# Another order of the attention stage's work items, in a kernel of attention and a routed feed-forward layer

## What is computed

```python
q, k, v = x @ wq_w.T + wq_b, x @ wk_w.T + wk_b, x @ wv_w.T + wv_b     # to heads, then _rope(q), _rope(k)
k, v = repeat(k, 4), repeat(v, 4)                                     # 4 query heads share a key head
att = softmax(where(mask, q @ k.T / HD ** 0.5, -inf))
x = layernorm(x + (att @ v) @ cp_w.T + cp_b)
scores = sigmoid(x @ gate_w.T) + gate_b
weights, indices = top_k(scores, 4)                                   # weights divided by their sum
shared = silu(x @ w1_shared) * (x @ w3_shared) @ w2_shared
routed = sum_e probs_e * (silu((x @ w1_e) * (x @ w3_e)) @ w2_e)
x = layernorm(x + shared + routed)
```

## Time and profile before

| | us |
|---|---|
| median of three runs (lowest, highest) | 566.12 (565.82, 566.49) |
| the profiled execution | 566.13 |
| its span, first to last instruction | 564.4 |
| attention stage, to the last product with V | about 317.6 |
| TensorE (PE) busy in the span | 529.9 (94%) |
| VectorE (DVE) busy | 439.0 (78%) |
| ScalarE (ACT) busy | 369.7 (65%) |
| GpSimd (POOL) busy | 295.4 (52%) |

### The profile page before, as it was taken

One profiled execution on the slowest core, in us unless ns is written; L12 is line 12 of the kernel. 1 busy time (PEld: TensorE's weight loads), 2 busy tenths in 40 slices (PEclk: granted clock), 3 DMA queues, 4 the chain that ended last, 5 costly groups with the idle time before them and its releaser, 6 DMA issues.

```text
span 564.4 us, 12218 instructions
## 1 busy us (share of the span) xinstructions
PE 529.9 (94%) x3801; PEld 360.5 (64%) x3801; DVE 439.0 (78%) x1122; ACT 369.7 (65%) x831; POOL 295.4 (52%) x341
## 2 busy tenths in 40 slices
PE   8999999999999899989999898899999999999880
PEld 4646444445454354535433487799999999999760
DVE  2387989899889799999992269987787878785682
ACT  2444767787887598868688574467676767676132
POOL 5121231655313657358978773777544444545671
PEclk9999999999999899989999999999999999999996
DMA  5954174400632912321132541576444334320892
GB/s 145 172 72 58 30 194 132 83 4 20 99 82 64 210 37 60 64 78 60 41 124 76 164 139 40 166 247 209 153 134 134 112 117 127 117 88 6 315 355 74
DMA packets 53741, 64.95 MB, mean 115 GB/s; under 512 B 8123, under 2 KB 47438, under 8 KB 53680
## 3 DMA queue, kind: packets, MB, share of 16 engines
q1 hardware_dynamic: 45952, 46.45, 32.1%
q0 software_dynamic: 7104, 17.60, 8.9%
q10 hardware_dynamic: 624, 0.13, 0.1%
HBM read 32.49 MB, written 25.76 MB: 103 GB/s over the span
## 4 chain that ended last, share of the span: by engine, by line
PE 71%; DVE 13%; POOL 6%; issue 4%; ACT 2%; DMA 2%; SPq 1%; ACTq 0%; POOLq 0%; DVEq 0%
PE psH L1670 14%; PE psS L1475 10%; PE psO L1460 9%; PE psT L1445 8%; PE psS L1537 4%; POOL xs_scratch L753 3%; DVE MX L1139 3%; PE psG L1681 3%; PE psX L1638 3%; PE psS L1480 2%; PE psY L1693 2%; PE psY L1697 2%; PE psY L1694 2%; PE psY L1695 2%; PE psY L1696 2%
## 5 line engine op out<-in xcount | busy, mean ns | idle before, releaser
L878 ACT ACTIVATE prob<-psT 128x512 f32<-128x512 f32 (+3 forms) x384 | 167.4, 495 | 54.9 <-PE psT L1445 52.3
L1139 DVE TENSOR_REDUCE MX<-psS 128x1 f32<-128x512 f32 (+3 forms) x344 | 183.1, 595 | 11.8 <-PE psS L1480 6.0
L1475 PE MATMUL psS<-KS,QS 96*128 96x512 bf16 (+3 forms) x384 | 110.9, 330 | 4.9 <-DVE MX L1139 2.5
L824 POOL DMA_INDIRECT y_scratch<-ys,dst x80 | 77.9, 973 | 68.9 <-ACT ys L1033 54.0
L1445 PE MATMUL psT<-QS,KS 98*128 98x512 bf16 (+3 forms) x384 | 107.7, 330 | 1.8 <-DMA QS<-MT 0.9
L782 POOL TENSOR_SCALAR_AFFINE_SELECT prob<-prob 128x512 f32<-128x512 f32 x64 | 42.3, 663 | 98.1 <-ACT prob L878 97.9
L1460 PE MATMUL psO<-prob,V 128*32 128x512 f32 (+3 forms) x768 | 82.7, 505 | 1.1 <-POOL prob L782 1.0
L1670 PE MATMUL psH<-wU,xh 128*128 (+1 forms) x384 | 81.7, 334 | 0.1
L753 POOL DMA_INDIRECT xs_scratch<-x1row,slotu x64 | 65.7, 1026 | 26.9 <-issue 16.2
L1445 PEld LDWEIGHTS psT<-QS,KS 98*128 98x128 bf16 x384 | 33.9, 98 | 54.8 <-ACT prob L878 35.4
L1475 PEld LDWEIGHTS psS<-KS,QS 96*128 96x128 bf16 x384 | 37.4, 99 | 46.1 <-DVE MX L1139 23.7
(11 more groups left out here) (252 smaller groups left out, 1005.8 us busy)
## 6 DMA issues: line engine op xcount, KB each, us to landing
xs<-xs_scratch SPq DMA_DIRECT2D x80, 134.0 KB
y<-y_scratch SPq DMA_DIRECT2D x16, 512.0 KB, 10.8
QS<-qp SPq DMA_DIRECT2D x48, 128.0 KB, 5.1
wU_raw<-in_L_ffn_w_routed_dram SPq DMA_DIRECT2D x32, 176.0 KB, 3.6
xs_scratch<-padrow SPq DMA_DIRECT2D x1, 2144.0 KB
xs_scratch<-padrow SPq DMA_DIRECT2D x16, 134.0 KB
x1row<-in_L_attn_x_dram SPq DMA_DIRECT2D x4, 512.0 KB, 6.8
out_dram<-x1row SPq DMA_DIRECT2D x8, 256.0 KB, 2.8
```

Of the source, the lines that this page charges most:

```text
L824: nc.gpsimd.indirect_dma_start(y4_dram, bass.IndirectOffsetOnAxis(ap=dst[:, n % NSEL, t:t + 1], axis=0), ys[:, n % NYS, t, :], None, bound ...
L878: nc.scalar.activation(prob[:, step % NPROB, h, 0:HALF - c0], ps[:, 0:HALF - c0], ACT.Exp).then_inc(s_Tfree, 1)
L1139: nc.vector.tensor_reduce(out=MX[:, c0 // HALF, heads[0]:heads[-1] + 1, i - TH * q], in_=src, op=ALU.max, axis=AX_X).then_inc(s_Sfree, 1)
L1475: last = mm(ps[:, e * dist:e * dist + cols], QS[0:ROWS, QAT[(k // 2) % NSLOT], g % 2 * G + h, (i - TH * q) * P:(i - TH * q + 1) * P], KS[b ...
```

## The change

The nine lines of ORDER are replaced by nine others. The new string has the same letters in the same numbers, so the same 1079 items run, each stream in its own order; the interleaving is another nearly everywhere. No other line of the kernel differs, and the expert stage has the same instructions in the same order.

```diff
 ORDER = """
-aaaaaaaadadpaaldppdlpdaaaapalaaaaapaapamalpppaxxaaaxxaaxaalxxxaaxxvamaxxavxxxaaaxavaxaxpaxmaxaxaaxxaaxvxaaaxxaexpavmaaxx
+aaaaaaaaddalplaadppplaaapaaaaapaaadapaampppaxaaxaxxaaaxxaxaxaxxldvaxmaalxvxaxxaaaxaxxxavvxxewaaaxaxaxvxaawxmxaaxaxapaasd
...
 """
```

More of the change, by code:

```diff
@@ L128 @@
 ORDER = """
-aaaaaaaadadpaaldppdlpdaaaapalaaaaapaapamalpppaxxaaaxxaaxaalxxxaaxxvamaxxavxxxaaaxavaxaxpaxmaxaxaaxxaaxvxaaaxxaexpavmaaxx
[L130 to L137, removed]
+aaaaaaaaddalplaadppplaaapaaaaapaaadapaampppaxaaxaxxaaaxxaxaxaxxldvaxmaalxvxaxxaaaxaxxxavvxxewaaaxaxaxvxaawxmxaaxaxapaasd
+xavvaaxaxxalamwxaxaxaxaaxvadxaenxxaxlavaxxaxadaaxvxaxsaxxaaxavvxaxaxaexaaxpawspmaaaxdvxaxxnaxaxvxxxaaadaawxvvasxxaaxaxaa
+xasxaxnepaaavvxxaaxaaxxaxavxxaaaxaxnxpxwxavaaxraxdaamxavaxxaaaxxvdxaaxaraxxaxaxaxvvxaalexxwaaaxaxavxaaxxaxrxaxwasawxrvvx
+xxaarxxaaxvxamaaxaxanxxaxrvaxxaaaxsvvaaxxxaaxaxaaxvraaxaxxrxeaxaxaoxrvvxlaxxaaarxraaxsxavvaxxaaaxaxrwaraxmaaxxaxaxxvwvlx
+axaxaxarraxxaaxvvwxamxaxaroxaxxraexrxxvvsvxxxanaxxnxaxrxxvxmxwaaxxovxcaxxaxaaxxcxavxxlaaxcxwvvxaaxcaxeaxaxamnasxxxvvarar
+aacaxacxvxaxxaaaxxacaxaxrmxrvexaxxorxawaxxvvxxaaaxraraxxraxxarcxawcvraxvxaaxexrxrxaaxvaxrraxaxaxvlvaxxamcxanxaxxvaaxacxa
+raxearnxaasxvaaaxcxovxxwaaxaxxrscaasnaxaxxavrvexxaacacaxcxvxxwxvxxxanxaxrxaxrcvscraxaxvxxaacrxraxarawxxxaavmaxaaxsaxvrac
+axxaarxrxxsaxaavrvcxaaarreaxxsccaracrvaxxraaxsaxavwxaxaaaxrarvaxaamxaaxacxcxaasxcaxavaaxaxaxaxaraxcarxccwxvxxxvsxxccaxwa
+axvxaxxrxxveaxaxxccvxaxxvxxxvxxawacxxcaxaxxvxnmcxxvxxxcvxxxxxvcxxxrxvexxnxvxxxvxxxxcxoccccnccxxvxxcxcvxxxvxxxxxxsvvvsen
 """
```

## The result

The changed kernel took 577.98 us (median of four runs, 576.22 to 579.88), the kernel before 566.31 beside it. The ratio is 1.018, with a 95% interval from 1.013 to 1.024. The predicted time was 568.0 with a range to 572.0: the sign was right, the size was not. The profiled execution took 576.22 us with a span of 574.5.

The account below looks back on a forecast made before the run. The prediction took TensorE as the bound, with its waits and half-clock stretches the only thing an order changes. Gains of -8.8 us and costs of +10.7 summed to +1.9, from 566.1 to 568.0 us; range 561.5 to 572.

Parts of the forecast that it names:

- What bounds the kernel: TensorE, busy 529.9 of 564.4 us; an order can only change the time it waits or runs at half clock.
- Group 1's M: At 50.00 us: its small DMA, now ahead of qload 2, should take group 0's 2.6 us: -0.9.
- Group 3's M behind the pad rows: Group 3's scores wait 5.1 us for the small DMA queued behind pad rows, plus 1.4 of half clock: +6.5.
- The rule weighed: DMA descriptors are consumed in ring order, so group 3's wait is 5.1 us, 6.5 with clock; without it 561.5.
- the queue doesn't bite: Rival: group 3's small DMA gets past the pad rows, without the 6.5 us; total 561.5, chance 0.15.
- qload 6: Group 12's scores at 191.04: more TensorE items cover the load, shrinking the wait and removing half clock: -3.1.
- M of group 5: At 103.91 us: no L803 near group 5's last maximum any more, so its wait goes: -1.2.
- The route item: Second token group, 245.62 us: only one wU difference near it now, so wait and half clock go: -3.1.
- The meetings of L803: GpSimd's L803 holds VectorE at maxima of groups 6, 13, 14 and third rank: +2.4, from 0 to 6.
- slower by more: Rival: L803 meetings at group 14's last maximum and one other place cost +6.2, not +2.4; 571.8, chance 0.12.
- The shorter leads: M of group 13, its result's copy and third token group's first output transpose have less cover: +1.0, 0 to 2.
- The end: End of the attention stage: one more GpSimd scatter before the last cut, +1.3, with smaller terms: +0.8 in sum.

Follow-up runs that it names:

- the pair on one chip: Changed order as it is, 575.53 us, and with group 12's first score block moved earlier on TensorE, 577.98 us; the kernel before ran at 565.10.
- The experiment: Changed order with the split item (0,0,1) moved right behind the third split copy: 572.30 us, against 566.48 for the kernel before.
- the kernel with both edits: Changed order with the pad rows behind group 3's small DMA of M and split (0,0,1) right behind the third split: 566.14 us (before 566.35).
- group 12 earlier: Changed order with group 12's first score block three transposed scores and two products earlier: 601.00 us (before 599.55), on another chip 577.98 (before 565.10).
- the last version: Kernel with scatters in GpSimd's idle time (554.77), plus moves of ScalarE's wA copy, group 13's result copy and group 15's M: 553.98 us (before 565.10).
- group 12's blocks later: Kernel before with group 1's M ahead of qload 2 and group 12's first three score blocks three to four TensorE items later: 597.62 us (before 598.46).

## Why the prediction was wrong, step by step

- **What bounds the kernel** was right: TensorE runs the same 3801 matmuls, and the lag, its waits and half-clock stretches, makes +10.0 of the 10.1 us between the two spans.
- **Group 1's M** (-0.9): right, measured -1.0, and the same in the order of before.
- **Group 3's M behind the pad rows** (+6.5): right in every link, and shown by four edits; mis-sized by 1.5. The wait was 6.25 us and not 5.1, just over the bound of 6 that the text gave for a slow load, and the half clock behind it cost 1.8 and not 1.4. The term that was off is the rate of qload 3's transfers: 173 GB/s was taken from two us in the earlier trace rows, and 117 was found. Why one stretch has the one rate and one the other, no run asks.
- **The rule weighed** (ring order) agrees with what was measured, and the rival "the queue doesn't bite" is out: 6.25, 3.02 and no wait for 2144, 1072 and 0 KB ahead.
- **qload 6** (-3.1): right, for the right reason, the distance: 3.7 us in the traces of the pair on one chip. My experiment on its place in SP's queue was a mistake that the prediction had not made.
- **M of group 5** (-1.2), and the stretch from 60 to 215: -7.0 in all instead of -4.3. The wait for group 5's M is gone. The surplus of 2.7 us stays unexplained: between 84 and 186 us the trace of before has no other wait of TensorE over 0.05 us, so it lies in distances a little over the shortest, and I have not taken it apart.
- **The route item** (-3.1): went as said, no L1189 over 1 us, but a part of it came back at M of group 13 just behind (L1147 2.33 us, and 0.88 us of TensorE's wait at 249.56).
- **The meetings of L803** (+2.4): the step that failed most, together with the end. The prediction took the length of L803, 1.7 us, as the most that a meeting can hold VectorE, and took half of before's loss. VectorE instructions of 2.33, 2.28, 1.94 and 1.53 us came. Those of 2.33 and 2.28 are longer than any L803; the runs show for the 2.28 that the L803 behind a scatter holds VectorE from within the scatter (0.17 us with L803 not ready, 1.02 with one scatter less ahead). The 1.94 is a plain meeting, 0.42 of its own and 1.5 of hold, and the 1.53 was none with L803 at all. The rival "slower by more" named the place, the last maximum of group 14, and it happened there; behind it the clock was at half for some six us, where the +2.4 held half of one of 3.4 us.
- **The shorter leads** (+1.0): none of the three places shows a wait over 0.2 us in after. The 0.88 us behind M of group 13 is for a bank, with VectorE held.
- **The end** (+0.8): GpSimd's scatters ahead of the cuts cost 1.12 and 0.66 us there, and M of group 15 1.39. The last product with V came at 327.1 us where the prediction had 319. By how much the order of GpSimd's work at the end matters is shown by the 6.4 us, half clock included, that two pairs of scatters and one normalisation brought.
- **The start** (0): missed. I had looked at what each DMA and each matmul waits for, but not at the counts. The wait of GpSimd's L767 is on a number of copies, and the item that brings the number had moved by sixteen places. The experiment gave 3.9 us, 1.6 of them by a half clock that comes in some executions and not in others.

Set beside the sum of +1.9: the start 3.5, group 3 1.5, the stretch at the end 4.6, the route item 1.3, less 2.7 in the middle, make the +10.0. The sign that came out is no proof of the sum: the change forecast, +1.9, is smaller than either of the two largest errors, 3.5 at the start and 4.6 at the end.

## What to carry to other kernels

When an order changes, list for every wait on a count which item brings that count in the new order; an item can wait for one that stands far behind it. A large DMA that nobody waits for belongs behind each small one that somebody does wait for, on the same queue: its price here was its bytes over the rate of the queue (332 GB/s), and the transfers ahead of it had a rate of their own (117). And an engine that has slack on average (GpSimd, 52%) still sets the pace where its work stands in a crowd ahead of the one piece that is waited for; look for its idle time just ahead of the crowd.

## What the runs showed of the hardware

- A VectorE instruction of 0.17 us that starts within a scatter (L753) of GpSimd is held to the end of the L803 behind that scatter (2.28 us), though it starts 0.54 us ahead of it. Where that L803 isn't ready, it takes 0.17. The Trainium skill, page "SBUF — State Buffer", section "SBUF: two separate sides", says of a VectorE instruction with two inputs in SBUF, as this one, and a GpSimd one that reads SBUF, that whichever starts first gets the ports that both share; here the later by the trace's starts won.
- The same wait of TensorE at the same place is followed by full clock or by half clock, and for different times. L1475 of group 15, with 1.78, 1.79 and 1.77 us of wait ahead, started at 273.30 in after, at 262.12 in the kernel with both edits, and at 277.01 in the changed order with group 12 earlier; a window of eight us in each:

```profile
272.00:280.00 8.00, 6.70 (x24) 2.63 (x28) 6.67 (x16) 4.35 (x9) 3.49 (x3) 0.60 0.43 127
```

```profile
262.00:270.00 8.00, 7.83 (x41) 3.33 (x41) 6.87 (x17) 5.20 (x11) 4.23 (x4) 0.79 0.45 127
```

```profile
277.00:285.00 8.00, 7.93 (x56) 4.58 (x57) 7.91 (x18) 5.61 (x12) 4.70 (x5) 1.00 0.45 130
```

The mean granted clock is 0.60, 0.79 and 1.00, of stretches at 0.50 and at 1.00. Even two executions of the changed order differ, behind the wait of 1.06 us at 41: 0.57 and 1.00 from 41 to 45 us, 1.6 us of lag apart. What decides it, the rows don't show.
- Two of the chips used ran the kernels 4 to 6% slower (598.46 and 599.55 us for before instead of 566, 584.69 instead of 553.98 for the last version, 601.00 instead of 577.98 for group 12 earlier). Three times in the expert stage no engine is busy there for 1.3 to 1.6 us (at 370, 394 and 417 us in the kernel before with group 12's blocks later), where before and the last version have no such stretch on the other chips, and once ScalarE stood for 3.96 us at 286, released by nothing on this core that the profile names. Its cause is open.
